# Feature sums of the third layer as fp32r matmuls over rounded halves, with both halves of the mapped keys as one 128-column stationary operand

## The reference, cut to what matters

```python
def _L2_xattn_ref(Q, K, V, projection):        # Q: layernorm(x); K and V: the context; projection: 64 x 256
    inv_sqrt_d = 1.0 / math.sqrt(d_model)
    rf_q = jnp.exp(jnp.einsum('bld,md->blm', Q * inv_sqrt_d, projection)) / math.sqrt(m)
    rf_k = jnp.exp(jnp.einsum('bld,md->blm', K * inv_sqrt_d, projection))
    KV = jnp.einsum('blm,bld->bmd', rf_k, V)
    Z = jnp.sum(rf_k, axis=1)
    out = jnp.einsum('blm,bmd->bld', rf_q, KV)
    normalizer = jnp.einsum('blm,bm->bl', rf_q, Z) + EPS
    return out / normalizer[..., None]
```

## Time and profile before

| | |
|---|---|
| median of 3 runs | 1699.77 us (1699.31 to 1701.76) |
| the profiled execution, its own time | 1695.96 us |
| its span in the trace | 1694.2 us |
| TensorE matmuls busy | 1589.8 us (94%) |
| TensorE weight loads busy | 1365.8 us (81%) |
| VectorE / ScalarE / GpSimd busy | 61% / 56% / 41% |
| mean granted TensorE clock | 0.973 of full speed |
| last layer before the edited one ends, the next begins | 1109.9 us, 1164.9 us |

### The profile page before, as it was taken

The page is one execution under the profiler, slowest core; times in us unless marked ns, Lnnn a source line. Parts: engine busy times, 40 slices in busy tenths (PEclk is TensorE's granted clock), DMA queues, the critical chain, the costliest instruction groups (busy, mean ns, idle before and its releaser), DMA issues. The chain is left out here.

```text
span 1694.2 us, 48950 instructions
## 1 busy us (share of the span) xinstructions
PE 1589.8 (94%) x20162; PEld 1365.8 (81%) x20179; DVE 1028.5 (61%) x1430; ACT 948.1 (56%) x1834; POOL 696.4 (41%) x625
## 2 busy tenths in 40 slices
PE   6999999999887999999999987998799999999987
PEld 5898888888666889988888775976488898888863
DVE  7667787885356777777777343012676666666623
ACT  4677777777413466665666712321267777777752
POOL 5655555551004645555554000000275555555302
PEclk9999999999987899999999999999999999999999
DMA  6675555554135666555564352971375555555440
GB/s 178 168 197 128 125 135 134 130 123 107 57 116 125 173 182 169 143 143 137 141 148 123 84 205 102 341 264 40 101 169 150 139 133 131 123 138 130 105 117 4
DMA packets 149248, 235.46 MB, mean 139 GB/s; under 512 B 24200, under 2 KB 64516, under 8 KB 148100
## 3 DMA queue, kind: packets, MB, share of 16 engines
q1 hardware_dynamic: 141090, 225.09, 50.7%
q10 hardware_dynamic: 7938, 7.23, 1.6%
HBM read 107.06 MB, written 0.23 MB: 63 GB/s over the span
## 5 line engine op out<-in xcount | busy, mean ns | idle before, releaser
L1305 DVE TENSOR_REDUCE L_xattn_maxima<-L_xattn_ps 128x4 f32<-128x1024 f32 x588 | 691.5, 1219 | 326.5 <-PE L_xattn_ps L877 322.6
L1067 ACT ACTIVATE L_xattn_p_ring<-L_xattn_ps 128x512 f32<-128x512 f32 x1176 | 674.2, 598 | 344.6 <-PE L_xattn_ps L926 329.4
L926 PE MATMUL L_xattn_ps<-L_xattn_q_packed,L_xattn_k_packed 128*128 128x256 f32 x2352 | 452.5, 298 | 10.0 <-ACT L_xattn_p_ring L1067 5.0
L926 PEld LDWEIGHTS L_xattn_ps<-L_xattn_q_packed,L_xattn_k_packed 128*128 128x128 f32 x2352 | 335.9, 190 | 71.6 <-issue 36.1
L962 PE MATMUL L_xattn_ps<-L_xattn_p_ring,L_xattn_v_ring 128*17 128x128 f32 x9408 | 289.3, 273 | 1.0 <-ACT L_xattn_p_ring L1067 1.0
L845 PE MATMUL L_xattn_ps<-L_xattn_ctx_halves,L_xattn_w_halves 128*128 128x256 f32 x1764 | 264.2, 288 | 0.9 <-POOL L_xattn_ctx_halves L1224 0.9
L962 PEld LDWEIGHTS L_xattn_ps<-L_xattn_p_ring,L_xattn_v_ring 128*17 128x17 f32 x9408 | 242.4, 97 | 23.5 <-ACT L_xattn_p_ring L1067 1.6
L849 PE MATMUL L_xattn_ps<-L_xattn_w_halves,L_xattn_ctx_halves 128*128 128x256 f32 x1764 | 260.5, 286 | 0.0
L1239 POOL TENSOR_TENSOR L_xattn_k_ring<-L_xattn_k_full,consts 128x512 fp32r<-128x512 f32 x147 | 156.1, 1062 | 222.1 <-ACT L_xattn_k_full L1080 112.5
L1221 POOL TENSOR_TENSOR L_xattn_ctx_halves<-L_xattn_ctx_chunk,consts 128x512 fp32r<-128x512 f32 x129 | 134.2, 1040 | 266.1 <-DMA L_xattn_ctx_chunk<-in_ctx_chunks 184.5
L845 PEld LDWEIGHTS L_xattn_ps<-L_xattn_ctx_halves,L_xattn_w_halves 128*128 128x128 f32 x1764 | 236.1, 196 | 4.3 <-issue 2.2
(11 more groups left out here) (378 smaller groups left out, 1142.2 us busy)
## 6 DMA issues: line engine op xcount, KB each, us to landing
L_xattn_k_packed<-L_xattn_k_ring SPq DMA_DIRECT2D x588, 128.0 KB, 2.4
L_xattn_ctx_chunk<-in_ctx_chunks SPq DMA_DIRECT2D x147, 256.0 KB, 3.2
L_xattn_k_packed<-L_xattn_k_ring SPq DMA_DIRECT2D x588, 64.0 KB, 2.2
L_ffn_W<-in_experts_W SPq DMA_DIRECT2D x16, 1024.0 KB, 13.8
L_xattn_mask_chunk<-L_xattn_mask ACTq DMA_DIRECT2D x49, 128.0 KB, 3.0
weights<-in_pack_L_attn SPq DMA_DIRECT2D x10, 512.0 KB, 4.1
L_xattn_ctxT<-in_ctxT SPq DMA_DIRECT2D x5, 896.0 KB, 10.2
L_xattn_ctx<-in_ctx SPq DMA_DIRECT2D x5, 896.0 KB, 9.1
```

The source lines that it names most:

```text
L926: last = pe.matmul(L.ps[:, bank, d * 2 * S:(d + 1) * 2 * S], self.k_packed[s][:, quarter, d, half * P:(half + 1) * P], q[:, 2 * pair:2 * p ...
L1067: act.activation(self.p[t % P_RING][:, 4 * quarter:4 * quarter + 4, :], L.ps[:, E_BANK[unit], :].rearrange("p (h n) -> p h n", n=S), ACT.Exp)\
L1305: dve.tensor_reduce(out[:, 4 * v:4 * v + 4], L.ps[:, M_BANK + 2 * v:M_BANK + 2 * v + 2, :] .rearrange("p b (k n) -> p (b k) n", k=2), AX_X ...
```

## The change

A value is split into a part rounded to fp32r and the remainder, also fp32r, so that products of halves can be formed by fp32r matmuls. In the edited layer only (a new class `SplitFeatureSums`; the shares in the two earlier layers keep `FeatureSums`):

- ScalarE copies each chunk's context (128x1792) into fp32r, VectorE subtracts this from the context and has the remainder, also 128x1792. Two buffers (`ctx_parts`).
- ScalarE copies the exponentials (128x448) into fp32r, VectorE makes their remainder. Both stand side by side for each tile, 64 + 64 columns (`rf_parts`).
- The sums are two fp32r matmuls for each tile: stationary 128x128 (both halves of the features), moving 258 columns of the context's rounded half, then of its remainder. PSUM bank 7 then has 128 rows, of which the lower 64 belong to the features' remainder.
- `add` adds the upper 64 rows and copies the lower 64 into the new rows 64 to 127 of `net.kv`. The projection is stored twice side by side, so the query features come out on 128 rows, and the last matmul contracts over 128 rows, which adds both parts. The logits still use the first 64 columns.
- The reload of a `ctx` slot waits for VectorE's remainder of the chunk that had it (`ctx_lo_ready`) instead of its sums. Rounding chunk i waits for the sums of chunk i-2.
- On VectorE the rotation's angles come behind chunk 1, its factors behind chunk 4.
- The packed projection has 128 instead of 64 columns for each half of the features, 128 KB instead of 64 for each of the three loads.

```diff
-    "L2_xattn": [("projection", DC * 64)],
+    "L2_xattn": [("projection", DC * 128)],
...
-        self.kv = ctx.enter_context(nc.sbuf_tensor("feature_sums", [64, D + 1], F32))
+        self.kv = ctx.enter_context(nc.sbuf_tensor("feature_sums", [P, D + 2], F32))
...
-                                 self.projection[:, e, :], start=k == 0 and e == 0, stop=e == 1, skip_group_check=True)
+                                 self.projection[:, e, 0:M], start=k == 0 and e == 0, stop=e == 1, skip_group_check=True)
...
+class SplitFeatureSums(FeatureSums):
+    PARTS = 2
+    def __init__(self, L):
+        super().__init__(L)
+        sb, n = L.sb, self.TILES
+        self.ctx_parts = [sb(f"ctx_parts{c}", [P, 2, n, D + 2], F32R) for c in range(self.PARTS)]
+        self.rf_parts = [sb(f"rf_parts{c}", [P, n, 2, self.M], F32R) for c in range(2)]
+    def load(self, sp, i):
...
+        if i >= self.RING:
+            sp.wait_ge(L["logits_in_psum"], i - self.RING + 1)
+        sp.dma_start(self.ctxT[c][:, :, :], ctxT[:, :, m * n * P:(m + 1) * n * P]).then_inc(L[f"ctxT_loaded{c}"], 16)
+        if i >= self.RING:
+            sp.wait_ge(L["ctx_lo_ready"], i - self.RING + 1)
+        sp.dma_start(self.ctx[c][:, :, 0:D], ctx[:, m * n:(m + 1) * n, :]).then_inc(L[f"ctx_loaded{c}"], 16)
+    def gpsimd(self, pool):
+        L = self.L
+        for c in range(self.PARTS):
+            pool.memset(self.ctx_parts[c][:, 0, :, D:D + 1].bitcast(F32), 1.0).then_inc(L["feature_ones_ready"], 1)
+            pool.memset(self.ctx_parts[c][:, 0, :, D + 1:D + 2].bitcast(F32), 0.0).then_inc(L["feature_ones_ready"], 1)
+            pool.memset(self.ctx_parts[c][:, 1, :, D:D + 2].bitcast(F32), 0.0).then_inc(L["feature_ones_ready"], 1)
+    def round_context(self, act, i):
+        L, c = self.L, i % self.PARTS
+        self.wait_loaded(act, "ctx", i)
+        if i >= self.PARTS:
+            act.wait_ge(L["chunk_summed"], i - self.PARTS + 1)
+        act.activation(self.ctx_parts[c][:, 0, :, 0:D], self.ctx[i % self.RING][:, :, 0:D], ACT.Copy)\
+           .then_inc(L["ctx_hi_ready"], 1)
+    def context_rest(self, dve, i):
+        L, c = self.L, i % self.PARTS
+        dve.wait_ge(L["ctx_hi_ready"], i + 1)
+        if i >= self.PARTS:
+            dve.wait_ge(L["chunk_summed"], i - self.PARTS + 1)
+        dve.tensor_tensor(self.ctx_parts[c][:, 1, :, 0:D], self.ctx[i % self.RING][:, :, 0:D],
+                          self.ctx_parts[c][:, 0, :, 0:D].bitcast(F32), ALU.subtract).then_inc(L["ctx_lo_ready"], 1)
+    def exponents(self, act, i):
...
+        act.activation(self.rf[i % 2][:, :], L.ps[:, 6, 0:self.TILES * self.M], ACT.Exp, scale=D ** -0.5)\
+           .then_inc(L["rf_ready"], 1)
+        act.wait_ge(L["rf_ready"], i + 1)
+        act.activation(self.rf_parts[i % 2][:, :, 0, :], self.rf[i % 2][:, :].rearrange("p (k m) -> p k m", m=self.M),
+                       ACT.Copy).then_inc(L["rf_hi_ready"], 1)
+    def features_rest(self, dve, i):
...
+        dve.tensor_tensor(self.rf_parts[i % 2][:, :, 1, :], self.rf[i % 2][:, :].rearrange("p (k m) -> p k m", m=self.M),
+                          self.rf_parts[i % 2][:, :, 0, :].bitcast(F32), ALU.subtract).then_inc(L["rf_lo_ready"], 1)
+    def sums(self, pe, i):
...
+        pe.wait_ge(L["ctx_lo_ready"], i + 1)
+        pe.wait_ge(L["rf_lo_ready"], i + 1)
+        for k in range(self.TILES):
+            for half in range(2):
+                last = pe.matmul(L.ps[:, 7, 0:D + 2], self.rf_parts[i % 2][:, k, :, :].rearrange("p a m -> p (a m)"),
+                                 self.ctx_parts[c][:, half, k, :], start=False, stop=True, skip_group_check=True)
+        last.then_inc(L["chunk_summed"], 1)
+    def add(self, dve):
+        L, M, kv, part = self.L, self.M, self.net.kv, self.L.ps[:, 7, 0:D + 1]
+        dve.wait_ge(L["chunk_summed"], self.count)
+        dve.tensor_tensor(kv[0:M, 0:D + 1], kv[0:M, 0:D + 1], part[0:M, :], ALU.add)
+        dve.tensor_copy(kv[M:2 * M, 0:D + 1], part[M:2 * M, :]).then_inc(L["kv_ready"], 1)
...
 class FeatureAttention:
...
     def tensor(self, pe):
...
-            last = pe.matmul(L.ps[0:M, 3, 0:S], proj[:, c, :], self.norm.xnT[:, c, :], start=c == 0, stop=c == 1)
+            last = pe.matmul(L.ps[:, 3, 0:S], proj[:, c, :], self.norm.xnT[:, c, :], start=c == 0, stop=c == 1)
...
     def scalar(self, act):
+        f.round_context(act, 0)
         f.exponents(act, 0)
         self.norm.scalar(act)
+        f.round_context(act, 1)
         f.exponents(act, 1)
...
         for i in range(2, f.count):
+            f.round_context(act, i)
             f.exponents(act, i)
             if i == 3:
                 self.turn.scalar(act)
...
     def vector(self, dve):
-        self.turn.vector_angles(dve, o)
-        self.turn.vector_factors(dve, o)
+        for i in range(self.features.count):
+            self.features.context_rest(dve, i)
+            self.features.features_rest(dve, i)
+            if i == 1:
+                self.turn.vector_angles(dve, o)
+            if i == 4:
+                self.turn.vector_factors(dve, o)
         self.features.add(dve)
```

More of the change, by code:

```diff
@@ L1660, in __init__ @@
         self.ctx = ctx.enter_context(nc.sbuf_tensor(f"{layer}_held_ctx", [P, self.TILES, D + 1], F32))
-        self.projection = ctx.enter_context(nc.sbuf_tensor(f"{layer}_held_projection", [P, DC, self.M], F32))
+        self.projection = ctx.enter_context(nc.sbuf_tensor(f"{layer}_held_projection", [P, DC, 2 * self.M], F32))
         self.loaded = [nc.alloc_semaphore(f"{layer}_held_{n}_loaded") for n in ("projection", "ctxT", "ctx")]
@@ L1690, in __init__ @@
         self.rf = [L.sb(f"rf{c}", [P, self.TILES * self.M]) for c in range(2)]
-        self.projection = self.held.projection if self.held else L.sb("projection", [P, DC, self.M])
+        self.projection = self.held.projection if self.held else L.sb("projection", [P, DC, 2 * self.M])
     def load_projection(self, sp):
@@ L1771, in add @@
     def add(self, dve):
-        L, kv, part = self.L, self.net.kv[:, :], self.L.ps[0:self.M, 7, 0:D + 1]
+        L, kv, part = self.L, self.net.kv[0:self.M, 0:D + 1], self.L.ps[0:self.M, 7, 0:D + 1]
         dve.wait_ge(L["chunk_summed"], self.count)
@@ L1779, in add @@
         dve.wait_ge(L["kv_ready"], 1)
+class SplitFeatureSums(FeatureSums):
[6 more added lines that the diff above has]
+    def load(self, sp, i):
+        if i == 0 and self.held:
+            return
+        L, n, c = self.L, self.TILES, i % self.RING
+        m = self.first + i
+        ctxT = self.net.ins["ctxT"].rearrange("(c p) t -> p c t", p=P)
+        ctx = self.net.ins["ctx"].rearrange("(j p) d -> p j d", p=P)
+        if i >= self.RING:
[25 more added lines that the diff above has]
+    def exponents(self, act, i):
+        L = self.L
+        act.wait_ge(L["logits_in_psum"], i + 1)
+        if i >= 2:
+            act.wait_ge(L["rf_lo_ready"], i - 1)
+            act.wait_ge(L["chunk_summed"], i - 1)
+        act.activation(self.rf[i % 2][:, :], L.ps[:, 6, 0:self.TILES * self.M], ACT.Exp, scale=D ** -0.5)\
[4 more added lines that the diff above has]
+    def features_rest(self, dve, i):
+        L = self.L
+        dve.wait_ge(L["rf_hi_ready"], i + 1)
+        if i >= 2:
+            dve.wait_ge(L["chunk_summed"], i - 1)
+        dve.tensor_tensor(self.rf_parts[i % 2][:, :, 1, :], self.rf[i % 2][:, :].rearrange("p (k m) -> p k m", m=self.M),
+                          self.rf_parts[i % 2][:, :, 0, :].bitcast(F32), ALU.subtract).then_inc(L["rf_lo_ready"], 1)
+    def sums(self, pe, i):
+        L, c = self.L, i % self.PARTS
+        if i == 0:
+            pe.wait_ge(L["feature_ones_ready"], 3 * self.PARTS)
+        pe.wait_ge(L["ctx_lo_ready"], i + 1)
[10 more added lines that the diff above has]
+        dve.tensor_copy(kv[M:2 * M, 0:D + 1], part[M:2 * M, :]).then_inc(L["kv_ready"], 1)
@@ L2198, in __init__ @@
         sb, M = L.sb, self.M
-        self.features = FeatureSums(L)
+        self.features = SplitFeatureSums(L)
         self.turn = TurnFactors(L)
-        self.rf_q = sb("rf_q", [M, S])
+        self.rf_q = sb("rf_q", [2 * M, S])
         self.norm_col = sb("norm_col", [S, 2])
@@ L2232, in tensor @@
         pe.wait_ge(L["rf_q_ready"], 2)
-        pe.matmul(L.ps[:, 5, 0:D + 1], self.rf_q[:, :], self.net.kv[:, :], start=True, stop=True)\
+        pe.matmul(L.ps[:, 5, 0:D + 1], self.rf_q[:, :], self.net.kv[:, 0:D + 1], start=True, stop=True)\
           .then_inc(L["y_in_psum"], 1)
@@ L2237, in scalar @@
         L, M, f = self.L, self.M, self.features
+        f.round_context(act, 0)
         f.exponents(act, 0)
         self.norm.scalar(act)
+        f.round_context(act, 1)
         f.exponents(act, 1)
         act.wait_ge(L["q_in_psum"], 1)
-        act.activation(self.rf_q[:, :], L.ps[0:M, 3, 0:S], ACT.Exp, scale=D ** -0.5).then_inc(L["rf_q_ready"], 1)
+        act.activation(self.rf_q[:, :], L.ps[:, 3, 0:S], ACT.Exp, scale=D ** -0.5).then_inc(L["rf_q_ready"], 1)
```

(2 more changed lines are left out.)

## The result

The changed kernel takes 1687.94 us (median of 4 runs, 1685.21 to 1688.73), the kernel before beside it 1699.54 us (4 runs, 1697.89 to 1701.76): ratio 0.9924, 95% interval 0.9902 to 0.9946. The forecast of 9.4 us less is a ratio of 0.9945, at the interval's upper end; 11.6 us less were measured. The profiled execution took 1688.73 us with a span of 1686.9, so 7.3 us less span than before.

| | before | after | changed kernel again (e1) |
|---|---|---|---|
| second group's cross-attention | 457.5 | 454.4 | 455.7 |
| **third group's cross-attention (edited)** | **54.0** | **43.9** | **44.2** |
| fourth group's cross-attention | 429.9 | 431.8 | 432.0 |
| last feed-forward layer, to the end of the span | 35.0 | 37.9 | 37.9 |

What follows compares the result with a forecast made beforehand. TensorE was taken to bound the edited layer: gains 1.37 + 6.0 + 2.47, minus 0.1 and 0.4, made 9.3, called 9.4 us; 1699.8 - 9.4 = 1690.4 us. Own range 1688.5 to 1692.5, wider range 1687.2 to 1694.6.

Steps and rivals of the forecast that it cites:

- The logits keep their 64 moving columns (the slice 0:M) and their price: In the edited layer's chunks, the logits block would stay at 3.26 us.
- Blocks 1 to 4, 4 x 1.50: Four steady sums blocks would each fall from 3.19 to 1.69 us, 6.0 us gained together.
- Bound and mechanism: TensorE sets the edited layer's end; one-pass fp32r sums records 0.1205 us apart replace f32 records 0.228 us apart; chance 0.80.
- up to the start of logits(2): First sums block, partly at the lower clock: 1.37 us gained, with the clock's rise at about 1124.1.
- the 0.1 at logits(5): Stall of 0.1 us or none before chunk 5's logits, waiting for the exponential behind ScalarE's rotation work.
- from there to VectorE's add: End of the last logits to VectorE's add: 6.41 us before, 3.94 after, 2.47 gained.
- the copy: At the layer's end, a second VectorE instruction for the lower 64 rows costs 0.4 us more.
- The last stall: Before the last sums block, the chain of exponential, rounding and remainder takes 2.00 us against 1.69: stall 0.3 us.
- Transfers: Chunk loads at 372 GB/s, 2.47 us each; last context lands at 1143.2, harmless up to about 1145.3.
- ScalarE and VectorE: New rounding and remainder work per chunk, 2.80 us on ScalarE and 2.65 on VectorE, under TensorE's period of 4.95.
- Rival 4: Clock falls to 1.2 GHz after the first sums block and stays: a chunk costs 8.9 us, 1712 us total; chance 0.03.

Runs made afterwards that it cites:

- e1: The changed kernel run again, unaltered, for more runs and a second trace: 1689.95 us, ratio 0.9938.
- e4: The changed kernel with 64 instead of 128 stationary columns in the sums, leaving out the features' remainders: 1693.35 us in one run.
- e12: The changed kernel with the sums' matmuls reading the same halves as f32 instead of fp32r: 1728.17 us in one run, layer 76.1 us.
- e3: The changed kernel with eight matmuls of zeros filling TensorE's wait for the second chunk's keys: 1685.64 us, ratio 0.9919, layer 43.4 us.
- e6: The changed kernel with VectorE's subtraction for the context done twice per chunk: 1691.3 us in one run, layer 51.0 us.
- e5: The changed kernel with 130 instead of 258 moving columns in the sums: 1707.34 us in one run, layer 67.1 us.
- e10: The changed kernel with 194 instead of 258 moving columns in the sums: 1711.21 us in one run, layer 65.2 us.
- e2: The kernel before with only the projection stored and loaded twice side by side: 1700.32 us, ratio 0.9996, layer 54.0 us.
- e9: The changed kernel with 130 moving columns in the sums and eight matmuls of zeros in the wait for keys: 1705.66 us in one run, layer 59.2 us.
- e11: The changed kernel with the second chunk's keys loaded a layer earlier and the last chunk's context handled in two pieces: 1685.78 us, ratio 0.9914.
- e7: The changed kernel with the context's reload waiting for the sums again, as before the change: 1686.8 us in one run, layer 43.9 us.
- e8: The changed kernel with the second chunk's keys loaded in the layer before: 1686.63 us, ratio 0.9924, layer 41.6 us.

## Where the prediction failed, and what of it held

The forecast was 1690.4 us, with 1688.5 to 1692.5 as its own range; 1687.94 us were measured, 0.6 us below that range, though inside the wider one (1687.2 to 1694.6). What failed is a term of the sum. The mechanism held.

- **The step that failed: "The logits keep their 64 moving columns (the slice 0:M) and their price", and with it "Blocks 1 to 4, 4 x 1.50".** The price of the logits was not kept: a block fell from 3.26 to 3.04 us, and five of them gave 1.1 us that the sum put at nothing. The sums gave 1.42 us a chunk and not 1.50, since their block is 1.77 us and not 1.69 (e4's block with a shorter load is 1.68, so 0.09 goes with the wider load). A chunk gave 6.45 - 4.81 = 1.64 us. Nothing in the logits changed, so some 0.2 us of the 3.26 belonged to the passage from and to the f32 sums of 64 stationary columns. The trace of before shows the loads of a logits block taking as long as after (3.20 us; after, 3.21 to 3.22), but with an idle time ahead of them:

```profile
1132.62 3.20 PEld L1745 LDWEIGHTS L_xattn_ps<-L_xattn_held_projection,L_xattn_ctxT 128*128 128x128 f32 x28 [0.39 <-issue]
```

  After, loads are busy 22.29 of 22.40 us. e12 says that it isn't the f32 format alone (3.07) and e4 that it isn't the 64 columns alone (3.04, 1133.81 to 1136.85). Whether both together make it was not tried, so the cause stays open. A price read as the pace between two kinds of block belongs to the pair.
- **Bound and mechanism: right.** TensorE sets the layer's end to within half a microsecond, one-record matmuls replace two-record ones (e12), and the clock and the loads don't stop it. Step by step in the two traces, with the forecast in brackets: up to the start of logits(2) 1.61 us (1.37; the clock came back some 1.7 us into the first sums block, not 2.1, an estimate from the windows); from there to the end of the last logits 29.10 - 22.45 = 6.65 us (5.9, with the 0.1 at logits(5)); from there to VectorE's add 6.41 - 4.13 = 2.28 us (2.47); the copy -0.39 (-0.4). Sum 10.15 (9.3), which is 54.05 - 43.90.
- **The last stall: right.** 0.29 us at sums(6), forecast 0.3, by the chain named. At logits(5) there was some 0.1 us (0.1).
- **Transfers: in hand less than forecast.** From the second chunk's keys (1113.50) to the last context (1141.72) eleven landings took 28.22 us instead of 27.2; TensorE was to have 2.1 us in hand and had 0.5: e3 took the clock's fall away and met them after 0.5 us. The rate wasn't lower than forecast: the queues moved 381 GB/s where 372 was taken.

```profile
1126.00:1141.00 15.00, 15.00 (x132) 14.88 (x131) 8.82 (x14) 11.60 (x15) 0.00 (x0) 1.00 1.07 381
```

```profile
1130.98 3.11 SPq L191 DMA_DIRECT2D weights<-in_pack_L_attn  x1
```

  Over the whole 28.22 us it was 381 GB/s too, 10.75 MB, and the eleven transfers are 10.09 MB. The forecast left out the second line: 1282 KB of weights for the next layer are issued behind the last context and share the queues with it. By the bytes moved since the layer's start, an estimate, 0.9 MB of them had gone when the last context landed. Whether they delayed it isn't shown: no run held them back, and the last six transfers took 2.43 us each (1127.14 to 1141.72) while the first context came 3.37 us behind its keys (1116.87). The Trainium skill (DMA: Bandwidth & Descriptors, "Where 436 GB/s comes from") gives about 358 GB/s as the limit of the memory side for one core; the trace doesn't agree, with 381 over 28 us.
- **ScalarE and VectorE: right to 0.02 us**: 1.70 (1.69), 0.55, 0.58 (0.56), 2.03, 0.62. e6 shows where a slower VectorE would have cost time: at sums(2) and (6).
- **Rival 4: wrong for this kernel, but nearer than 0.03 suggests.** Against it stood a window of logits at clock 1.00. e5 and e10 show such logits with thinner sums at the lower clock all through, at 8.96 us a chunk. The prediction had no row on what width of the sums keeps the clock, so that it didn't decide here is in part luck.
- **The number:** 11.6 us less against 9.4. Some 0.8 of the 2.2 us are in the layer, as above. The other 1.4 were seen in no trace: outside the edited layer the traces of the kernel before and of e2 took 1640.2 and 1639.8 us, the two of the changed kernel 1643.0 and 1645.5. In e1 the gain by the ratio is 10.5 us. That the rest is scatter of the medians fits both intervals, and is argued, not shown.

## What to carry to other kernels

Replacing a two-record f32 matmul by two one-record fp32r matmuls over rounded halves pays when the halves can share one stationary operand and idle engines can do the rounding: here 10 us for 17 us on each of two engines. A forecast should ask for the price of the blocks beside the changed one too, since it can move with them. After such a change look for the next bound at once, by removing the biggest remaining loss and seeing which wait takes its place; here half a microsecond lay between TensorE and the transfers. Look also at what is issued behind the stage's last transfer. And ask of every stage that gets thinner what it does to the granted clock: less work in one block cost half the speed of all the others in e5 and e10.

## What the runs showed of the hardware

- TensorE can be busy all the time and stay at 1.2 GHz: 41.7 us in e5 (130 moving columns) and 44.5 us in e10 (194), with the same 64-column logits that run at 2.4 GHz when the sums have 258. The Trainium skill (TensorE: Matmul & The Clock Gate, "Why this matters for your kernels") tells to keep idle gaps out; e9 had no idle over 0.61 us in the 15 us ahead of its fall and none after it, and spent 32 us at the lower level, so the absence of gaps was not enough here.
- At the lower clock fp32r records of 130, 194 and 258 moving columns keep nearly the same pace, 3.03, 3.08 and 3.14 us for 14 (e5, e10, e6), with load records of 333, 334 and 330 ns: there the load, not the columns, seems to set it. No run varied the load at that clock.
- The clock falls in logits(1) in some executions and in logits(0) in others, though e4 and e12 run the changed kernel's code up to the first sums. It then stayed low for some 13.7 us instead of 6.8 (e4, e11, e12), which cost e4 some 2 us (45.6 against 43.9).
- One core's queues moved 378 to 381 GB/s over 26 to 28 us in five traces (the changed kernel, e1, e3, e7, e8).
